# A sparse graph layer pair on one core: the tail chunk gathered fifth, node tiles summed in PSUM banks of their own, and a new order in the softmax tail

## The reference

```
agg[i] = sum_j adj[i,j] * x[j] * T[i,j]
r, z   = sigmoid(agg Wi + bi + x Wh + bh)        n = tanh(agg Wi_n + bi_n + r * (x Wh_n + bh_n))
x1     = layernorm(x + (1 - z) * n + z * x)
h      = x1 W (4 heads of 32);  e[i,j] = leaky_relu(a_dst.h[i] + a_src.h[j]) where adj > 0
out    = layernorm(x1 + softmax(e) h)
```

## Time and profile before

| | |
|---|---|
| median of 3 runs | 59.25 us (59.2 to 59.4) |
| the profiled execution | 59.2 us, its span 57.5 us |
| PE busy | 44.1 us, 77% of the span |
| DVE busy | 38.3 us, 67% |
| ACT busy | 23.6 us, 41% |
| POOL busy | 12.1 us, 21% |
| granted PE clock, mean | 0.964 |

### The profile page before, as it was taken

One profiled execution on the slowest core, in us unless ns is written; L12 is line 12 of the kernel. 1 busy time (PEld: TensorE's weight loads), 2 busy tenths in 40 slices (PEclk: granted clock), 3 DMA queues, 4 the chain that ended last, 5 costly groups with the idle time before them and its releaser, 6 DMA issues.

```text
span 57.5 us, 1459 instructions
## 1 busy us (share of the span) xinstructions
PE 44.1 (77%) x530; PEld 34.8 (60%) x530; DVE 38.3 (67%) x152; ACT 23.6 (41%) x58; POOL 12.1 (21%) x24
## 2 busy tenths in 40 slices
PE   0599697976999999899957969869699999940000
PEld 0143376755987983688947758768679897820000
DVE  3985989999953494302388339963799186999630
ACT  1804456469993360023940066942950380000200
POOL 1940002757777771000000500000000000000000
PEclk9999999999999999999999999999999999999555
DMA  0698980031212221000000000000000131000033
GB/s 0 147 315 281 397 301 22 6 63 29 57 46 60 66 66 49 0 0 0 0 0 0 0 0 11 0 0 6 0 0 13 44 94 43 11 0 0 11 95 93
DMA packets 3001, 3.34 MB, mean 58 GB/s; under 512 B 544, under 2 KB 2080, under 8 KB 2992
## 3 DMA queue, kind: packets, MB, share of 16 engines
q1 hardware_dynamic: 2560, 2.62, 14.3%
q0 software_dynamic: 288, 0.59, 4.2%
q10 hardware_dynamic: 144, 0.00, 0.1%
HBM read 2.69 MB, written 0.26 MB: 51 GB/s over the span
## 4 chain that ended last, share of the span: by engine, by line
DVE 37%; PE 18%; POOL 11%; issue 9%; DMA 8%; ACT 6%; SPq 5%; DVEq 1%; POOLq 0%; ACTq 0%
POOL edge L336 11%; PE bank L648 6%; PE bank L728 6%; SPq L300 5%; DMA edge<-in_L_gnn_edge_table,eidx 5%; DMA x1n<-x 4%; DVE colhot L975 4%; DVE x L1097 2%; ACT h_parts L447 2%; DVE st L1108 2%; DVE x1n L1213 2%; PE bank L631 2%; DVE h_parts L1144 2%; DVE y L1101 2%; DVE yT L1066 2%
## 5 line engine op out<-in xcount | busy, mean ns | idle before, releaser
L336 POOL DMA_INDIRECT edge<-in_L_gnn_edge_table,eidx x9 | 9.2, 1025 | 9.0 <-DVE eidx L983 6.9
L585 PE MATMUL bank<-x_parts,colhot 128*128 128x128 bf16 x108 | 7.4, 218 | 0.0
L774 PE MATMUL bank<-h_parts,colhot 128*128 128x128 bf16 x108 | 7.0, 218 | 0.0
L585 PEld LDWEIGHTS bank<-x_parts,colhot 128*128 128x128 f16 x108 | 6.5, 97 | 0.4
L774 PEld LDWEIGHTS bank<-h_parts,colhot 128*128 128x128 f16 x108 | 6.3, 96 | 0.3
L975 DVE TENSOR_TENSOR colhot<-bank,slot_mid 128x512 f16<-128x512 f32 x8 | 5.3, 684 | 0.2 <-PE bank L555 0.2
L648 PE MATMUL bank<-ones_adj 128*128 128x512 f16 x8 | 3.6, 628 | 2.1 <-DVE ones_adj L928 2.1
L728 PE MATMUL bank<-xr,eprod 128*128 128x128 f32 (+1 forms) x24 | 4.3, 302 | 0.2 <-DVE eprod L1130 0.2
L555 PE MATMUL bank<-rowhot,posm 128*128 128x128 f16 (+1 forms) x48 | 3.6, 208 | 1.0 <-DVE colhot L975 0.5
L728 PEld LDWEIGHTS bank<-xr,eprod 128*128 128x128 f32 (+1 forms) x24 | 3.3, 188 | 1.6 <-issue 0.6
L832 PE MATMUL bank<-vals,xr 128*128 128x132 f32 (+1 forms) x24 | 3.9, 309 | 0.0
(11 more groups left out here) (176 smaller groups left out, 92.1 us busy)
## 6 DMA issues: line engine op xcount, KB each, us to landing
adj_t<-in_adj_turned SPq DMA_DIRECT2D x3, 256.0 KB, 4.5
adj_i<-in_adj_first SPq DMA_DIRECT2D x1, 256.0 KB, 2.8
x_parts<-in_x SPq DMA_DIRECT2D x1, 256.0 KB, 4.3
xT<-in_x_turned SPq DMA_DIRECT2D x1, 256.0 KB, 4.8
x1n<-x SPq DMA_DIRECT2D x4, 64.0 KB, 2.5
out<-out_sb SPq DMA_DIRECT2D x2, 128.0 KB, 2.1
whhT<-in_L_gnn_w_hh SPq DMA_DIRECT2D x1, 192.0 KB, 4.9
wT<-in_L_gnn_w_ih SPq DMA_DIRECT2D x1, 192.0 KB, 4.9
```

Of the source, the lines that this page charges most:

```text
L336: nc.gpsimd.indirect_dma_start(out=edge[:, c], out_offset=None, in_=edge_table, in_offset=bass.IndirectOffsetOnAxis(ap=eidx[:, c:c + 1], a ...
L585: nc.tensor.matmul(x_bank[k % 2][:, i * P:(i + 1) * P], cols_at(jb, c), x3[:, s, jb], start=(jb == 0 and s == 0), stop=(jb == Q - 1 and s ...
L774: mm = nc.tensor.matmul(hg_at(c), cols_at(jb, c), h3[:, s, jb], start=(g == 0 and s == 0 and c % 4 == 0 and jb == 0), stop=False, skip_gro ...
```

## The change

- **Gather order.** Chunk 8 is selected, one-hot coded and gathered fifth, behind chunks 0 to 3, and before chunks 4 to 7. For this the hand-written lists of PE and DVE ahead of the branch are in another order. No instruction is added or taken away there.
- **Banks.** The two tiles of a half are summed in two banks (6 and 7); the four tiles of `scatter` in banks 2 to 5. All four or two chunks of 128 slots come first, then the tails, without the waits on `s_mixed`.
- **Softmax tail.** DVE does `normalise(1)` where `split_h(1)` stood and the other way round. On PE the last gathers are in another order. The 12 matmuls of `add_mean` are replaced by three adds on POOL (`h_sum`, fp32, 128x128) and one fp32 matmul. Of the four output groups ACT now writes two, from `neg_mean` that DVE makes, and stores them by a DMA of its own queue.

```diff
-ORDER = (0, 1, 2, 8, 3, 4, 5, 6, 7)
-IDX = ((0,), (1,), (2, 3), (4, 5), (6, 7), (8,))
+ORDER = (0, 1, 2, 3, 8, 4, 5, 6, 7)
+IDX = ((0,), (1,), (2, 3), (8,), (4, 5), (6, 7))
...
+            with pool.If(sparse == 1):
+                pool.wait_ge(s_h, 1)
+                nc.gpsimd.tensor_tensor(h_sum[:], h_parts[:, 0, 0], h_parts[:, 0, 1], ALU.add).then_inc(s_hsum, 1)
+                pool.wait_ge(s_h, 2)
+                for t in (2, 3):
+                    pool.wait_ge(s_hsum, t - 1)
+                    nc.gpsimd.tensor_tensor(h_sum[:], h_sum[:], h_parts[:, 0, t], ALU.add).then_inc(s_hsum, 1)
...
+            def last_norm():
+                act.wait_ge(s_nm, 1)
+                for n in range(2, Q):
+                    nc.scalar.activation(out_sb[:, n], y2[:, n], ACT.Identity, bias=neg_mean[:, n - 2:n - 1],
+                                         scale=rstd[:, n:n + 1]).then_inc(s_oa, 1)
+                act.wait_ge(s_oa, 2)
+                act.dma_start(out_v[:, 2:4], out_sb[:, 2:4]).then_inc(s_out, 16)
...
             base(2)
             index(0)
+            degrees(3)
             select(2)
-            index(1)
-            degrees(3)
-            select(3)
             ranks(3)
             base(3)
+            index(1)
+            select(3)
             hidden(2, bank[1], range(0, 1))
             select(4)
             hidden(2, bank[1], range(1, 2))
             index(2)
             select(5)
             hidden(2, bank[1], range(2, 3))
+            index(3)
             select(6)
             hidden(2, bank[1], range(3, 4)).then_inc(s_hnp, 1)
-            index(3)
             select(7)
+            index(4)
             source_rows(0)
             select(8)
-            index(4)
...
-                    for c, t in ((4 * g, 0), (4 * g + 1, 0), (4 * g + 2, 1), (MIX, 0), (4 * g + 3, 1), (MIX, 1)):
+                    for c in range(4 * g, 4 * g + 4):
                         pe.wait_ge(s_ep, ORDER.index(c) + 1)
-                        slots = slice(0, P) if c < MIX else part(2 * g + t)
-                        if c == MIX and t == 1:
-                            pe.wait_ge(s_mixed, g + 1)
...
+                    pe.wait_ge(s_ep, ORDER.index(MIX) + 1)
+                    for t in range(2):
+                        slots = part(2 * g + t)
+                        mm = nc.tensor.matmul(agg_bank[:, t], eprod[slots, MIX], rT_at(MIX)[slots], start=False,
+                                              stop=False, skip_group_check=True)
...
-                gather_h(1, 1, range(4, 8))
-                pe.wait_ge(s_hlo, 2)
-                for chunks in (range(4), (8,), range(4, 8)):
-                    gather_h(1, 2, chunks).then_inc(s_hg, 1)
-                add_mean(1).then_inc(s_meanp, 1)
+                pe.wait_ge(s_hlo, 2)
+                gather_h(1, 2, range(4)).then_inc(s_hg, 1)
+                gather_h(1, 2, (8,)).then_inc(s_hg, 1)
+                pe.wait_ge(s_hsum, 3)
+                pe.wait_ge(s_p512, 1)
+                nc.tensor.matmul(mean_bank, part512[:], h_sum[:], start=True, stop=True, skip_group_check=True)\
+                    .then_inc(s_meanp, 1)
+                gather_h(1, 1, range(4, 8))
+                gather_h(1, 2, range(4, 8)).then_inc(s_hg, 1)
...
             col_onehot(2)
             edge_index(1)
             row_onehot(2)
-            split_x(1)
-            col_onehot(3)
             keep_base(3)
             held_slots(3)
+            split_x(1)
+            row_onehot(3)
+            col_onehot(3)
             edge_index(2)
-            row_onehot(3)
             col_onehot(4)
+            edge_index(3)
             col_onehot(5)
+            col_onehot(6)
+            edge_index(4)
             split_x(2)
-            edge_index(3)
-            col_onehot(6)
             col_onehot(7)
-            edge_index(4)
             col_onehot(8)
             edge_index(5)
```

More of the change, by code:

```diff
@@ L126, in build_gnn @@
         x1n = sb("x1n", [P, Q, H])
-        part512 = sb("part512", [P, P], BF16)
+        part512 = sb("part512", [P, P])
+        h_sum = sb("h_sum", [P, H])
         eps_col = sb("eps_col", [P, 2])
+        neg_mean = sb("neg_mean", [P, 2])
         spread = sb("spread", [P, Q])
@@ L175, in build_gnn @@
         wa = wcat[:, H:H + 2 * NH]
-        bank = [ps(f"bank{k}", [P, 512])[:] for k in range(8)]
+        banks = ps("banks", [P, 8, 512])
+        bank = [banks[:, k] for k in range(8)]
         tiles4 = [b.rearrange("p (t h) -> p t h", t=4) for b in bank]
@@ L191, in build_gnn @@
         zT_bank = bank[2][0:16, :]
-        mean_bank = bank[5][:, 0:H]
-        num_bank = [bank[k][:, 0:2 * HV].rearrange("p (t f) -> p t f", t=2) for k in (2, 3)]
+        mean_bank = bank[6][:, 0:H]
+        num_bank = [banks[:, 2 + 2 * k:4 + 2 * k, 0:HV] for k in range(2)]
+        agg_bank = banks[:, 6:8, 0:P]
         def rows_of(t):
@@ L300, in _ @@
                 sp.dma_start(x1n[:, n], x1[n * P // Q:(n + 1) * P // Q]).then_inc(s_x1n, 16)
-            for k in range(2):
-                sp.wait_ge(s_o, 2 * k + 2)
-                sp.dma_start(out_v[:, 2 * k:2 * k + 2], out_sb[:, 2 * k:2 * k + 2]).then_inc(s_out, 16)
+            sp.wait_ge(s_o, 2)
+            sp.dma_start(out_v[:, 0:2], out_sb[:, 0:2]).then_inc(s_out, 16)
             sp.wait_ge(s_out, 32)
@@ L458, in keep_agg @@
                     act.wait_ge(s_agg, g + 1)
-                    nc.scalar.copy(aggT[:, 2 * g:2 * g + 2].rearrange("h t p -> h (t p)"), bank[6][:, 0:2 * P])\
+                    nc.scalar.copy(aggT[:, 2 * g:2 * g + 2], agg_bank)\
                         .then_inc(s_aggT, 1)
@@ L479, in _ @@
                 deviation(2)
+                last_norm()
             with act.Else():
@@ L576, in source_rows @@
                 i = XGROUP[k].index(c)
-                pe.wait_ge(s_col, c + 1)
+                pe.wait_ge(s_col, ORDER.index(c) + 1)
                 pe.wait_ge(s_xlo, 1)
@@ L777, in gather_h @@
                     return mm
[L779 to L785, removed]
                 pe.wait_ge(s_h, 1)
@@ L835, in _ @@
                 pe.wait_ge(s_emp16, 1)
+                pe.wait_ge(s_zd, 1)
                 for t in range(Q):
                     nc.tensor.matmul(num_bank[t // 2][:, t % 2, H:HV], ident16[:], empty16[:, t:t + 1].broadcast_to([P, NH]),
-                                     start=(t % 2 == 0), stop=False, skip_group_check=True)
+                                     start=True, stop=False, skip_group_check=True)
                 pe.wait_ge(s_vals, 1)
-                for c in range(3):
+                for c in range(4):
                     scatter(c, c // 2)
                 pe.wait_ge(s_vals, 2)
[L843 to L847, removed]
-                pe.wait_ge(s_vals, 3)
[L849 to L854, removed]
+                for t in range(Q):
+                    mm = scatter(MIX, t)
+                mm.then_inc(s_num, 1)
+                pe.wait_ge(s_vals, 3)
+                for c in range(4, 8):
+                    mm = scatter(c, c // 2)
+                mm.then_inc(s_num, 1)
             with pe.Else():
@@ L1116, in finish @@
                 dve.wait_ge(s_rstd, 3)
-                for n in range(Q):
+                nc.vector.scalar_tensor_tensor(neg_mean[:], mv[:, 2:4, 0], -1.0, rstd[:, 2:4], ALU.mult, ALU.mult)\
+                    .then_inc(s_nm, 1)
+                for n in range(2):
                     nc.vector.tensor_scalar(out_sb[:, n], y2[:, n], mv[:, n, 0:1], rstd[:, n:n + 1],
@@ L1165, in _ @@
                 split_u(1)
-                split_h(1)
+                normalise(1)
                 dve.wait_ge(s_z, 1)
@@ L1175, in _ @@
                                         headmask[:].unsqueeze(2).broadcast_to([P, Q, NH]), ALU.mult).then_inc(s_zs, 1)
-                normalise(1)
+                split_h(1)
                 dve.wait_ge(s_new, 1)
```

20 lines of the change are left out of this document (9 added, 11 removed).

## The result

| | before | after |
|---|---|---|
| median | 59.33 us (4 runs, 59.2 to 59.46) | 61.31 us (4 runs, 60.82 to 62.04) |
| ratio | | 1.031, 95% interval 1.026 to 1.036 |
| the profiled execution | 59.2 us, span 57.5 | 61.4 us, span 59.7 |
| mean granted PE clock | 0.964 | 0.916 |

A forecast was written before the change was run, and what follows sets the result against it. Bound by POOL's serial gathers, then both halves' gates, maximum scans, DVE's x1n wait and finish. Terms 2.12 - 0.87 - 0.61 + 0.09 - 0.06 = +0.67, absorbed 0.59, output -0.17: -0.09 on 59.2, so 59.1 us; range 58.5 to 59.9.

The forecast's parts named there:

- the walk: PE's and DVE's lists ahead of the branch, followed step by step with measured durations: first aggregate pass 2.1 us later, at 24.8.
- The rival: PE's new 1 us gap before source_rows(0): clock falls, next 3 us of work take twice as long, 62; chance 0.04 with other losses.
- Ahead of the branch, +2.1: PE's and DVE's reordered lists before the first aggregate: source_rows(0) 2.61 late, first pass 2.1 later; bounds 1.7 and 2.6.
- The two aggregates, -0.87 and -0.61: Both halves' aggregates on PE: full chunks first, tails side by side in two banks, 1.54 for 2.41 and 1.47 for 2.08.
- The rival that tails follow each other: In both aggregates tails still run in turn, +0.42 each: 59.9; chance 0.14.
- POOL's adds hold up DVE: 59.45: Rival at split_h(0): POOL's first add and DVE can't read SBUF side by side, DVE loses 0.35; chance 0.18.
- Softmax tail, the delay is absorbed: From normalise(1) to the x1n correction: +0.67 becomes +0.08, third product waits for PE, no wait for the x1n DMA.
- Output, -0.17: Four output groups shared by DVE and ACT: last DMA issued 0.17 earlier; bounds 0.3 gain and 0.2 loss.

The follow-up runs named there:

- the thin stretch filled: Changed kernel plus eight idle matmuls in PE's gaps between 11.5 and 16 us, the gap before source_rows(0) kept: 59.72 us, ratio 1.007.
- experiment 4: Changed kernel plus four idle matmuls, either inside select(4) (59.82 to 61.44 us) or from index(3) on (59.76 to 61.19 us).
- the front alone: Kernel before with only PE's and DVE's new lists ahead of the branch, chunk 8 gathered fifth: 62.98, 62.83, 62.85 and 61.39 us.
- experiment 3: Changed kernel plus idle matmuls: four in PE's gap before source_rows(0), 59.68 to 61.78 us; or eight between 11.5 and 16 us, 59.72 us.
- experiment 6: Changed kernel with the old lists ahead of the branch, POOL's first add released by x1 (57.40 us) or by the second yT (62.44 us, another chip).
- the filled gap: Changed kernel plus four idle matmuls in PE's gap before the first source_rows: 61.78, 59.68, 61.70 and 60.51 us.
- experiment 5: Changed kernel with DVE's split_x(2) moved ahead of edge_index(2): median 59.45 us, ten runs, 58.48 to 60.46.
- the late fills: Changed kernel plus four idle matmuls from index(3) on, 14 to 16.5 us, none inside select(4): 59.76, 59.86, 61.19 and 60.43 us.
- the last pair's moved add: Changed kernel with old lists ahead of the branch, POOL's first add released by the second yT: 62.44 us; kernel before on that chip 64.83 us.

## Why the prediction was wrong

**The clock, which the sum left out, is the step that failed.** The forecast gave the fall a chance of 0.04, so its sum held nothing for it. It cost 2.01 us: from `source_rows(0)` to the first aggregate pass it is 9.51 in the changed kernel (17.35 to 26.86) and 7.50 where the clock holds (17.84 to 25.34 with the thin stretch filled; 7.51 in both profiled kernels of experiment 4). The forecast looked at the one new gap and asked whether gaps had hurt before (the longest of the front before was 0.54, one of 1.00 came later, and the clock was full through both). In the profiled run the fall came 0.9 us before that gap. That PE's work ahead of the dense part gets thinner could be read from the walk: the dense work begins 2.67 us later, and PE's busy time from 5 us to there grows only from 7.79 to 8.42 us (ahead of `source_rows(0)` stand one index group more than before, not two as I wrote above, and 16 small selects in place of four matmuls). That the clock would fall for it no row of before could say. The rival had the right outcome by the wrong cause, and its 62 is near the measured 61.3 by luck: it took 3 us of work at twice the time, and the clock was down for 6.8 us and cost 2.0. By their mean clocks all four runs of the changed kernel fell (0.915 to 0.936), and three of four of the front alone. Without the fall the same kernel would take an estimated 59.2 (experiment 3 less the delay by its fills) to 59.45 (59.2 + 2.17 - 1.92, by the terms below); this was not run without a fill. "No change" would then have been about right, at the upper side.

**Ahead of the branch, +2.1.** The walk of the lists held: `source_rows(0)` starts at 17.35 for 17.29, with 0.90 of idle time before it for "about 1 us". From there to the first aggregate pass it is 7.50 where the clock holds, for 8.00 before, so 0.50 comes off behind the split for the forecast's 0.49. At full clock the front costs 2.67 - 0.50 = 2.17, for 2.12.

**The two aggregates, -0.87 and -0.61.** By the timeline the first one goes from 26.86 to 28.41, 1.55 for 2.41 before: -0.86; the second from 34.58 to 36.05, 1.47 for 2.08: -0.61. The banks alone gave -1.6. The rival that tails follow each other is dead: in the changed kernel the tails of both tiles start together, the first passes at 27.92 and the second ones at 28.13 and 28.14, and all four take 0.49.

**POOL's adds hold up DVE: 59.45.** This rival's mechanism is there, at 0.14 us and not 0.35. The add and the second split, which take 0.46 and 0.42 alone, take 0.69 and 0.56 here. The Trainium skill (SBUF — State Buffer, "two separate sides") has the one that starts first hold the shared ports for its whole instruction, and the other wait. The trace agrees on who waits: the first split starts at 37.14, ahead of the add (37.19), and isn't longer; the second starts at 37.60, while the add runs until 37.88, and is. In experiment 6 the add starts first (35.40) and keeps its 0.46, and `g_t` (35.56) loses 0.16. The size is less than the whole add: by the rule the second split would wait until 37.88, 0.28 us, and it lost 0.14. Whether the two take turns inside the stretch that their records share, the profile doesn't show. The add itself takes 0.46 alone, in the middle of the forecast's bounds of 0.28 and 0.72; the estimate of 0.3 from the Trainium skill's GPSIMD Engine Reference (3.1) was too low.

**Softmax tail, the delay is absorbed.** +2.88 at the third product (49.94 for 47.06) is +2.31 at `x1n`: 0.57 for 0.59. The waits are the ones forecast: third product for PE, none for the DMA. Scatter's shortening was put at nothing; the tail alone, with the old scatter, has DVE wait 0.46 for it, so in this kernel it was needed.

**Output, -0.17.** It brought 0.04: `out_sb` started 2.30 late, and the last output DMA is issued 2.26 late. ACT's two groups take 0.88, not 0.63: with bias and scale an operation on SBUF data is 477 to 492 ns, where the scaled copies that I took the price from are 0.37.

The terms behind the front add up to -1.92 (from 4.18 late at the first pass to 2.26 late at the last DMA), for the forecast's -2.21: 0.14 is POOL's add, 0.13 the output. The miss of 2.3 us on the profiled execution is then 2.0 of the clock, 0.3 of these two and less than 0.1 of the front. But for the clock, the mechanism and nearly every size were right.

## What to carry to other kernels

An order that makes PE wait a little everywhere can cost twice: the waits, and then the clock under the work that was put off. Before a move that thins out PE, compare PE's busy time in windows ahead of its dense work, not only the longest gap; this warns, but doesn't decide. And read the clock of each run: a kernel that stands at the edge shows times that spread by 2 us, and the same schedule can look like a gain or a loss. Of a large change run the parts alone: here 1.9 us of gain stood behind 3.9 us of loss, and the version with the old front, 57.39 us, beats both.

## What was not expected of the hardware

- The granted clock fell to 1.2 GHz with no idle time of PE above 0.93 us ahead of it, and stayed up over an idle time of 1.00 us in the kernel before. Fills of the early half or of the late half each kept it in some runs; what exactly decides isn't settled. Busy sums don't tell alone: from 8 to 14 us PE was busy 4.78 before and 4.35 in the kernel of experiment 5, which lost its clock at 13.9; but the kernel with the late fills, with 4.33 there, kept it in its profiled run.
- In the changed kernel and in the profiled runs of the front alone, the filled gap and experiment 5 the fall lasted 6.8 us each time, and it began at 15.5, 15.5, 14.2 and 13.9 us. In the profiled run of the last pair's moved add it lasted 13.7.
- The clock row reads full from the start, but PE's first eight matmuls (128x512) take 3.49 us, 0.44 each. Fills of the same shape take 0.43 at a granted 0.50 and 0.22 at 1.00. So those first ones ran at the lower level, which the row doesn't show.
- The same program falls in some runs and not in others: front alone 61.39 us at a clock of 0.978, 62.85 at 0.897.
- The kernel before took 59.3 us in four batches and 64.8 in the fifth. The four batches of the experiments ran on four different chips; whether the chip is the reason wasn't tested.
- A POOL add of 128x128 costs a DVE operation with two SBUF inputs that starts while it runs 0.14 to 0.16 us (562 for 425 ns, 580 for 420). A DVE operation that started first lost nothing, and the add took 0.23 longer.
- Tails of 32 rows for two tiles in two banks start within 0.01 us of each other: four fp32 passes in 0.49 us, where one tail with its turn took 0.42 before.
